# Input loaded and normalised in two token halves on two engines, and half of a lookup table made later, in a three-layer fused kernel on one Trainium2 core

## The reference

```
xn = _layernorm(x)                      # per token, over the 128 channels
x + attn_block(xn) + two_layers(xn)
# attn_block: group norm over all tokens, q k v, decayed retention in 16 heads of 8, output
#             projection, then group norm, 128 -> 256 -> 128 with silu
# each of two_layers (8 heads of 64):
h = shift_token(x); q, k, v = split(h @ wqkv)
q = l2norm(q) * q_scale; k = l2norm(k) * k_scale
q, k = rotary_xpos(q, k)                # cos, sin and a position scale
o = local_attention(q, k, v)            # window of 64 and the one before
x = x + o @ wo
h = layernorm(shift_token(x)); a, g = split(h @ w1 + b1); x = x + (a * gelu(g)) @ w2 + b2
```

## Time and profile before

| what | us |
|---|---|
| median of 3 runs | 972.21 |
| lowest and highest run | 970.54, 973.97 |
| span of the profiled execution, first to last instruction | 969.5 |
| TensorE busy | 862.3 (89%) |
| ScalarE busy | 701.7 (72%) |
| VectorE busy | 634.5 (65%) |
| GpSimd busy | 631.0 (65%) |

### The profile page before, as it was taken

One profiled execution on the slowest core, in us unless ns is written; L12 is line 12 of the kernel. 1 busy time (PEld: TensorE's weight loads), 2 busy tenths in 40 slices (PEclk: granted clock), 3 DMA queues, 4 the chain that ended last, 5 costly groups with the idle time before them and its releaser, 6 DMA issues.

```text
span 969.5 us, 26414 instructions
## 1 busy us (share of the span) xinstructions
PE 862.3 (89%) x10836; PEld 580.5 (60%) x10836; DVE 634.5 (65%) x1082; ACT 701.7 (72%) x1449; POOL 631.0 (65%) x500
## 2 busy tenths in 40 slices
PE   0678889989899898998999989999999999999876
PEld 0345666666667666666566656565656565656552
DVE  5874666666667567576575776757575758575632
ACT  0446786977868779677797778787878787878651
POOL 4588677675876758667586665757575758585700
PEclk9979999999999999999999999999999999999997
DMA  9100000000000000000000000000000000000000
GB/s 295 30 1 3 1 2 2 3 3 2 2 3 1 3 1 1 3 2 3 1 2 3 1 2 2 1 21 4 17 7 23 2 23 2 21 3 24 1 23 11
DMA packets 20482, 13.47 MB, mean 14 GB/s; under 512 B 4579, under 2 KB 19597, under 8 KB 20237
## 3 DMA queue, kind: packets, MB, share of 16 engines
q1 hardware_dynamic: 15108, 10.49, 3.6%
q10 hardware_dynamic: 5256, 1.31, 0.7%
HBM read 9.70 MB, written 2.10 MB: 12 GB/s over the span
## 4 chain that ended last, share of the span: by engine, by line
PE 63%; ACT 15%; DVE 10%; issue 7%; POOL 3%; DMA 1%; DVEq 0%; POOLq 0%; SPq 0%; ACTq 0%
PE pQK L1181 8%; PE pS L1108 6%; PE pT L1093 5%; PE pT L1050 5%; PE pM L1125 5%; PE pV L1146 4%; PE pS L1082 4%; PE pM L1254 4%; DVE m L734 4%; PE pT L1237 3%; PE pQK L1345 3%; PE pM L1119 2%; PE pS L1069 2%; ACT prT L545 2%; ACT pr L598 1%
## 5 line engine op out<-in xcount | busy, mean ns | idle before, releaser
L366 POOL TENSOR_TENSOR rn<-rn,half_neg 128x16 f32<-128x16 f32 x64 | 187.5, 2929 | 5.3
L379 POOL TENSOR_TENSOR m<-m 128x1024 f32<-128x1024 f32 x64 | 150.9, 2358 | 0.0
L364 POOL TENSOR_SCALAR rn<-ss 128x16 f32<-128x16 f32 x64 | 16.3, 254 | 193.3 <-DVE ss L747 192.1
L386 POOL TENSOR_TENSOR qkn<-m,rn 128x1024 f32<-128x1024 f32 x64 | 121.7, 1902 | 5.0
L1181 PE MATMUL pQK<-wqkv,hT 128*128 128x512 f32 x256 | 123.6, 606 | 0.9 <-DVE m L734 0.9
L780 DVE TENSOR_REDUCE mx<-pS 128x8 f32<-128x1024 f32 x64 | 78.1, 1220 | 63.8 <-PE pS L1082 63.8
L561 ACT ACTIVATE sq<-pQK 128x1024 f32<-128x1024 f32 x64 | 65.4, 1022 | 25.5 <-PE pQK L1181 25.4
L747 DVE TENSOR_REDUCE ss<-sq 128x16 f32<-128x1024 f32 x64 | 77.6, 1213 | 6.7 <-ACT sq L561 6.4
L782 DVE TENSOR_TENSOR pr<-pS,mx 128x1024 f32<-128x1024 f32 x64 | 78.4, 1225 | 2.2
L521 ACT ACTIVATE kT<-pT 128x512 f32<-128x512 f32 x64 | 38.0, 595 | 57.3 <-PE pT L1050 56.8
L545 ACT ACTIVATE prT<-pT 128x1024 f32<-128x1024 f32 x64 | 65.0, 1016 | 15.6 <-PE pT L1093 14.8
(11 more groups left out here) (169 smaller groups left out, 2015.9 us busy)
## 6 DMA issues: line engine op xcount, KB each, us to landing
x<-in_L_attn_x SPq DMA_DIRECT2D x4, 512.0 KB, 9.4
xs<-in_L_attn_x SPq DMA_DIRECT2D x8, 256.0 KB, 2.8
out<-aqkT SPq DMA_DIRECT2D x8, 256.0 KB, 2.2
wqkv<-in_L_ffn_wqkv SPq DMA_DIRECT2D x2, 768.0 KB, 9.8
tab<-in_k_tab SPq DMA_DIRECT2D x1, 1024.0 KB, 10.4
w<-in_L_ffn_w SPq DMA_DIRECT2D x2, 341.0 KB, 10.5
wo<-in_L_ffn_wo SPq DMA_DIRECT2D x2, 256.0 KB
cst<-in_k_cst ACTq DMA_DIRECT2D x1, 404.5 KB, 4.3
```

The lines of the kernel that those rows point to most:

```text
L366: eng.tensor_tensor(rn[:, k % 2, :], rn[:, k % 2, :], half_neg[:, 0:2 * H], ALU.pow).then_inc(S["rn_done"], 1)
L379: eng.tensor_tensor(m1[:, k % 2, :], m1[:, k % 2, :], m2[:, :], ALU.add).then_inc(S["add_done"], 1)
L386: eng.tensor_tensor(qkn[:, k % 2, :].rearrange("p (h d) -> p h d", d=DH), m1[:, k % 2, :].rearrange("p (h d) -> p h d", d=DH), rn[:, k % 2 ...
```

## The change

x is loaded in eight transfers instead of four: the first four steps of each batch, then the last four. VectorE takes the statistics of the first half, joins them, then those of the second half. GpSimd's two halves of 1/sqrt stay. VectorE also makes `shift` = -mean/std (L1002 in the changed kernel), so that ScalarE can normalise as Identity(x * rstd + shift): of each step ScalarE now normalises batches 0 and 1, VectorE batches 2 and 3. ScalarE's copy of step t-1 out of PSUM follows its normalisation of step t. Layer 1's rotary table is no longer made in the opening: its q part is made on GpSimd before slot 2 of body (0,1), its k part before slot 2 of body (0,2); its gains have a tile of their own, and VectorE waits for all twelve instructions only in body (1,0). The statistics of xnT move on VectorE from before slot 0 to before slot 1 of body (0,0). The opening's loops are written out.

The core of the diff:

```diff
-        gain = hidden[:, MASK_END:MASK_END + DEPTH * 2 * DH].rearrange("p (l g d) -> p l g d", l=DEPTH, g=2)
+        gain = [hidden[:, MASK_END:MASK_END + 2 * DH].rearrange("p (g d) -> p g d", g=2), sb("gain1", [P, 2, DH])]
...
         @block.sync
         def _(sp):
-            for b in range(NB):
-                sp.dma_start(x[:, b, :, :], a["L0_attn_x"][b].rearrange("(t p) d -> p t d", p=P)).then_inc(x_ld[b], 16)
+            for h in range(2):
+                for b in range(NB):
+                    steps = slice(h * NT // 2, (h + 1) * NT // 2)
+                    sp.dma_start(x[:, b, steps, :],
+                                 a["L0_attn_x"][b].rearrange("(t p) d -> p t d", p=P)[:, steps, :]).then_inc(x_ld[h][b], 16)
...
-            for l in range(DEPTH):
-                for g in range(2):
-                    eng.tensor_tensor(rope[l][:, :, g, :], tab[:, :, g, :],
-                                      gain[:, l, g, :].unsqueeze(1).broadcast_to([P, NT, DH]),
+
+            def rotary_table(l, g):
+
+                eng.tensor_tensor(rope[l][:, :, g, :], tab[:, :, g, :],
+                                  gain[l][:, g, :].unsqueeze(1).broadcast_to([P, NT, DH]),
+                                  ALU.mult).then_inc(rope_done, 1)
+                for s in range(2):
+                    eng.tensor_tensor(rope[l][:, :, 2 + g, 32 * s:32 * s + 32], tab[:, :, 2 + g, 32 * s:32 * s + 32],
+                                      gain[l][:, g, 32 - 32 * s:64 - 32 * s].unsqueeze(1).broadcast_to([P, NT, 32]),
                                       ALU.mult).then_inc(rope_done, 1)
-                    for s in range(2):
-                        eng.tensor_tensor(rope[l][:, :, 2 + g, 32 * s:32 * s + 32], tab[:, :, 2 + g, 32 * s:32 * s + 32],
-                                          gain[:, l, g, 32 - 32 * s:64 - 32 * s].unsqueeze(1).broadcast_to([P, NT, 32]),
-                                          ALU.mult).then_inc(rope_done, 1)
+            rotary_table(0, 0)
+            rotary_table(0, 1)
 
             def body(new, old, ff):
                 for k in range(NB):
                     if k == 1 and new and is_start(new):
                         pool_group_norm(eng, 0)
+                    if new in ((0, 1), (0, 2)) and k == 2:
+                        rotary_table(1, new[1] - 1)
                     if new == (1, 0) and k == NB - 1:
                         pool_group_norm(eng, 1)
                     pool_slot(eng, new, old, ff, k)
...
-            with eng.Fori(0, NT // 2) as half:
-                for u in range(2):
-                    t = 2 * half + u
-                    eng.wait_ge(xnt_mm, t + 1)
-                    eng.activation(xnT[:, :, bass.ds(t * P + 1, P)], xn_banks[u][:, :].rearrange("p (b n) -> p b n", b=NB),
-                                   ACT.Copy).then_inc(xnt_ev, 1)
+
+            def keep_transposed(t):
+                eng.wait_ge(xnt_mm, t + 1)
+                eng.activation(xnT[:, :, t * P + 1:t * P + 1 + P], xn_banks[t % 2][:, :].rearrange("p (b n) -> p b n", b=NB),
+                               ACT.Copy).then_inc(xnt_ev, 1)
+            for t in range(NT):
+                eng.wait_ge(rstd_done, t // (NT // 2) + 1)
+                eng.wait_ge(shift_done, t // (NT // 2) + 1)
+                need(eng, xnt_mm, t - 1)
+                for b in range(NB // 2):
+                    eng.activation(xn[:, t % 2, b, :], x[:, b, t, :], ACT.Identity, bias=shift[:, t, b:b + 1],
+                                   scale=rstd[:, t, b:b + 1]).then_inc(xn_act, 1)
+                if t > 0:
+                    keep_transposed(t - 1)
+            keep_transposed(NT - 1)
             eng.wait_ge(memset_done, 7 + 4 * NB)
...
-            for b in range(NB):
-                eng.wait_ge(x_ld[b], 16)
-                with eng.Fori(0, NT // 4) as quad:
-                    for u in range(4):
-                        t = 4 * quad + u
+            def row_stats(h):
+                for b in range(NB):
+                    eng.wait_ge(x_ld[h][b], 16)
+                    for u in range(NT // 2):
+                        t = h * (NT // 2) + u
                         eng.bn_stats(xst[:, b, t, :], x[:, b, t, :]).then_inc(xst_done, 1)
-            eng.wait_ge(xst_done, NB * NT)
-            for t in range(NT):
-                for b in range(NB):
-                    eng.bn_aggr(mv[:, t, b, :], xst[:, b, t, :]).then_inc(st_done, 1)
+
+            def join_stats(h):
+                eng.wait_ge(xst_done, NB * NT // 2 * (h + 1))
+                for u in range(NT // 2):
+                    t = h * (NT // 2) + u
+                    for b in range(NB):
+                        eng.bn_aggr(mv[:, t, b, :], xst[:, b, t, :]).then_inc(st_done, 1)
+
+            def row_shift(h):
+                steps = slice(h * NT // 2, (h + 1) * NT // 2)
+                eng.wait_ge(rstd_done, h + 1)
+                eng.scalar_tensor_tensor(out=shift[:, steps, :], in0=mv[:, steps, :, 0], scalar=-1.0, in1=rstd[:, steps, :],
+                                         op0=ALU.mult, op1=ALU.mult).then_inc(shift_done, 1)
+
+            def normalize(t):
+                need(eng, xnt_mm, t - 1)
+                for b in range(NB // 2, NB):
+                    eng.tensor_scalar(xn[:, t % 2, b, :], x[:, b, t, :], mv[:, t, b, 0:1], rstd[:, t, b:b + 1],
+                                      ALU.subtract, ALU.mult).then_inc(xn_done, 1)
+            row_stats(0)
+            join_stats(0)
+            row_stats(1)
+            row_shift(0)
+            join_stats(1)
             eng.wait_ge(cst_ld, 32)
             eng.tensor_copy(mask16[:, :], mask32).then_inc(mask_done, 1)
-            eng.wait_ge(rstd_done, 1)
-
-            def normalize(half):
-                for u in range(2):
-                    t = 2 * half + u
-                    need(eng, xnt_mm, t - 1)
-                    for b in range(NB):
-                        eng.tensor_scalar(xn[:, u, b, :], x[:, b, t, :], mv[:, t, b, 0:1], rstd[:, t, b:b + 1],
-                                          ALU.subtract, ALU.mult).then_inc(xn_done, 1)
-            for half in range(NT // 4):
-                normalize(half)
-            eng.wait_ge(rstd_done, 2)
-            with eng.Fori(NT // 4, NT // 2) as half:
-                normalize(half)
-            eng.wait_ge(rope_done, 6 * DEPTH)
+            for t in range(NT // 2):
+                normalize(t)
+            row_shift(1)
+            for t in range(NT // 2, NT):
+                normalize(t)
+            eng.wait_ge(rope_done, 6)
 
             def input_stats():
 
@@ -1018,11 +1048,12 @@
             def body(new, old, ff):
                 for k in range(NB):
                     if new and is_start(new):
-                        if k == 0:
+                        if k == 1:
                             input_stats()
-                        if k == 1:
                             bias_into_ffn()
                             dve_group_norm(eng, 0, c("ng"), c("nb"))
+                    if new == (1, 0) and k == 0:
+                        eng.wait_ge(rope_done, 6 * DEPTH)
                     if new == (1, 0) and k == 1:
                         eng.wait_ge(A["cs"], NB * NT)
                         dve_group_stats(eng, 1)
@@ -1363,17 +1394,13 @@
                     mm = eng.transpose(pT[:, g * 512 + j * P:g * 512 + (j + 1) * P], araw[:, 4 * g + j, :], ident)
                 mm.then_inc(awt_mm, 1)
 
-            def transpose_normalized(half):
-                for u in range(2):
-                    t = 2 * half + u
-                    eng.wait_ge(xn_done, 4 * t + 4)
-                    need(eng, xnt_ev, t - 1)
-                    for b in range(NB):
-                        mm = eng.transpose(xn_banks[u][:, b * P:(b + 1) * P], xn[:, u, b, :], ident)
-                    mm.then_inc(xnt_mm, 1)
-            transpose_normalized(0)
-            with eng.Fori(1, NT // 2) as half:
-                transpose_normalized(half)
+            for t in range(NT):
+                eng.wait_ge(xn_done, 2 * t + 2)
+                eng.wait_ge(xn_act, 2 * t + 2)
+                need(eng, xnt_ev, t - 1)
+                for b in range(NB):
+                    mm = eng.transpose(xn_banks[t % 2][:, b * P:(b + 1) * P], xn[:, t % 2, b, :], ident)
+                mm.then_inc(xnt_mm, 1)
 
```

More of the change, by code:

```diff
@@ L146, in program @@
         rstd = sb("rstd", [P, NT, NB])
+        shift = sb("shift", [P, NT, NB])
         cbst = [sb("cbst0", [P, NB, 2, 6]), sb("cbst1", [P, NB, NT, 6])]
@@ L226, in score_bank @@
             return pQK[:, 512 * (b % 2):512 * (b % 2) + 512]
-        x_ld = [sem(f"x_ld{b}") for b in range(NB)]
+        x_ld = [[sem(f"x_ld{h}_{b}") for b in range(NB)] for h in range(2)]
         cst_ld, tab_ld, aw_ld, wqkv_ld, w1_ld, w_ld, gain_ld, col_ld = (
@@ L232, in program @@
         memset_done, mask_done = sem("memset_done"), sem("mask_done")
+        xn_act, shift_done = sem("xn_act"), sem("shift_done")
```

(2 more changed lines are left out.)

## The result

The changed kernel took 975.53 us (median of 20 runs, 971.84 to 978.22) against 971.88 for the kernel before (20 runs beside it): ratio 1.0038, 95% interval 1.0028 to 1.0047. The forecast was 975.9. The profiled execution has a span of 972.5 (before 969.5) at a mean granted clock of 0.981 (0.983). It is slower, by little over what can be told from no change.

The account below looks back on a forecast made before the run. TensorE, busy 89% of the span, bounds the bodies; VectorE, slowed beside GpSimd, paces the opening. Span 969.5 - 2.6 + 2.6 + 3.7 = 973.2, plus 2.7 to the median: 975.9 us, range 970.6 to 978.3.

Parts of the forecast that it names:

- The opening, -2.6: Normalising on ScalarE and VectorE at 1.35 us a step starts hT at 38.4 instead of 40.97: -2.6 us.
- The halves, 0: Loads and statistics of x in halves gain 0 +-0.5 us, since ScalarE cannot normalise before about 26.45 anyway.
- The statistics, +2.6: Group norm statistics behind slot 0 of body (0,0) make TensorE wait, giving back the opening's 2.6 us; second ss at 58.7.
- rival C: Denser transposes raise TensorE's clock in the opening, 1.9 us sooner to second ss, table paid: 974.0 us; chance 0.15.
- The table, +3.7: Layer 1's table ahead of slot 2 delays ars by 1.90 us, costing 1.8 to 1.9 per body, 3.7 for both.
- Rival B: Table hidden, as VectorE and TensorE catch up inside the retention; opening and statistics cancel: 972.2 us; chance 0.20.
- Rival D: Statistics stay covered, opening's gain carried through, second ss before 57: 968.7 us with table hidden, 970.6 half paid; chance 0.13.
- E: Rival: the eight x transfers delay ScalarE's queue by 1 to 2 us: 977.5 us; chance 0.07.
- 2.7 between span and median: Whole run: the median run lies 2.7 us above the profiled span, added to 973.2 to give 975.9.
- A: The forecast itself: opening -2.6, statistics +2.6, table +3.7: 975.9 us, own range 974.3 to 977.8; chance 0.45.

Follow-up runs that it names:

- kernel 5: Changed kernel with the statistics of xnT back ahead of slot 0 and layer 1's table ahead of slot 1: 969.31 us, ratio 0.9956.
- Kernel 8: Changed kernel with x loaded by four transfers instead of eight halves, statistics still in eight steps: 976.70 us, ratio 1.0046.
- 11: kernel 9 with x loaded by four transfers instead of eight: 964.47 us, ratio 0.9913.
- kernel 9: kernel 5 with the eight bias column loads issued by SyncE, behind its weight loads, instead of by ScalarE: 959.13 us, ratio 0.9871.
- kernel 1: Changed kernel with the statistics of xnT put back ahead of slot 0 of body (0,0): 973.48 us, ratio 1.0017.
- kernel 3: Kernel before with only layer 1's table moved, to ahead of slot 2 of bodies (0,1) and (0,2): 972.58 us, ratio 1.0015.
- kernel 4: Kernel before with only layer 1's table moved, to ahead of slot 1 of bodies (0,1) and (0,2): 967.99 us, ratio 0.9953.
- 12: kernel 9 with VectorE's wait for layer 0's rotary table moved behind the eight statistics rows: 960.20 us, ratio 0.9871.
- kernel 2: Changed kernel with layer 1's table made ahead of slot 1, not slot 2, of bodies (0,1) and (0,2): 971.83 us, ratio 1.0000.

## Why the prediction was right

- **The opening, -2.6: right.** It won 2.53. The step of ScalarE was 1.29 (1.35 forecast), the queue ended 0.40 later than I took it, and the two errors nearly cancel. In the runs kernel 5, which has this opening without the two late costs, is 3.9 us below the kernel before of its group (2.6 to 5.9 by its interval).
- **The halves, 0: right, and shown.** Kernel 8, and 11 against 9, show the cover and what lies under it: the eight loads bring nothing while ScalarE's queue runs to 24.5, and 4 to 5 us when it ends at 12.6.
- **The statistics, +2.6: right in kind, small by 0.5.** The second `ss` came at 59.24, not 58.7, so all of the opening and 0.5 more was lost up to there, 3.0; undoing the move gave 2.33 in the trace of kernel 1 and 2.05 in the runs. I had `gst` at 56.1, and it was at 56.62. The 0.5 is TensorE's, not the move's: q and k of slot 0 took 3.62 us, 0.75 more than the 2.87 of the earlier trace rows, and some 0.2 of it came back behind. The changed kernel's timeline:

```profile
39.21 2.04 PE L1177 MATMUL pV<-wqkv,hT 128*128 128x512 f32 x2 [1.30 <-ACT hT L510]
41.05 3.62 PE L1212 MATMUL pQK<-wqkv,hT 128*128 128x512 f32 x4
44.46 2.57 PE L1413 MATMUL pM<-col,w 128*128 128x1 f32 x24
```

  They began 2.5 us earlier and took 0.9 each to their end, against 1.88 for four at 2.4 GHz, so they ran at the lower level (1.2 GHz), although the profile lists a granted clock of 1.00 for 41 to 44.7 us: the clock rose no sooner, which is rival C the other way round. But one trace can't lay this to the denser transposes. Kernels 3 and 4 are the same code up to body (0,1), and differ as much (first 3, then 4):

```profile
40.17 2.99 PE L1187 MATMUL pQK<-wqkv,hT 128*128 128x512 f32 x4
```

```profile
39.99 3.62 PE L1187 MATMUL pQK<-wqkv,hT 128*128 128x512 f32 x4
```

  With the two-engine opening it was 3.10 and 2.99 in kernels 9 and 12, and 3.56 to 3.62 in the other seven profiles. The Trainium skill (TensorE: Matmul & The Clock Gate, "What's actually happening") has the clock rise after sustained activity; in none of these nine profiles did the denser transposes ahead bring it for v and all of q, k. The row that GpSimd's `qkn` had held for 1.03 took 0.16, as forecast, but another one, ahead of it, took 0.62 instead of 0.15 (54.11), as I had allowed.
- **The table, +3.7: right.** GpSimd's 1.90 is in the changed kernel and in 3, `aqk` waits 1.92 longer, and moving the table off that slot gave 3.7 (2) and 4.6 (3 to 4). But I had each body 1.8 longer, and in the profile body (0,1) is 1.37 longer and body (0,2) 1.41 (62.72 against 61.31): of the 1.9 at slot 2, 0.5 is given back to waits further on. Against kernel 2, which has the table at slot 1, they are 2.01 and 1.25 longer. So the traces have 2.8 to 3.3 for both bodies, and the runs 3.7 and more; no run settles the difference, which is no larger than what executions differ by. Rival B, a table that costs nothing, is out.
- **Rival D is out** (second `ss` at 59.24, not before 57), and so is E (the queue 0.4 later, 0.27 by kernel 8, and kernel 8 no faster).
- **That the total hit to 0.4 us** is partly luck. The change itself was forecast as +3.7 on 972.21 and measured as +3.65 on 971.88. But the forecast's 2.7 between span and median is no fixed cost of a run, as I took it: in every execution listed with its span the time is 1.7 to 1.9 above it, so 0.9 of the 2.7 was that profile's being faster than its median. (And the upper end of the range, 978.3, is 0.5 above the 977.8 of A that it was to be taken from.) Executions of the changed kernel lie up to 3.7 us from their median, and the trace shows one reason. Windows of the changed kernel, 109 to 113 and 113 to 124 us (columns: span of the window, busy time of PE, PEld, DVE, ACT and POOL, granted clock, DMA share, GB/s):

```profile
109.00:113.00 4.00, 4.00 (x46) 3.36 (x45) 1.56 (x2) 1.07 (x2) 3.35 (x2) 0.57 0.02 4
113.00:124.00 11.00, 11.00 (x118) 7.89 (x117) 7.72 (x9) 9.09 (x15) 6.08 (x4) 1.00 0.00 1
```

  TensorE is busy throughout the first window, yet its granted clock is 0.57, so most of it lies at the lower level (1.2 GHz). Just ahead of it TensorE had stood still for 2.13 us:

```profile
108.21 1.10 PE L1177 MATMUL pV<-wqkv,hT 128*128 128x512 f32 x2 [2.13 <-DVE xr L821]
```

  The kernel before and kernel 2 stand still for the same 2.13 us there and keep 1.00. From `rn` of slot 0 to `rn` of slot 1 of body (0,1), the changed kernel fell 1.6 us further behind the kernel before. The window from 68 to 72, which follows an idle of 3.41 (3.15 before), has 0.57 after and 1.00 before; kernel 3 has 1.00 and kernel 4 falls to 0.50 behind the same idle of 3.40, and from slot 2 to slot 3 of body (0,0) kernel 4, the same code so far, loses 1.6 us on kernel 3. So whether the clock falls behind such an idle differs by execution, and a single trace is no measure of 1 or 2 us between kernels.
- **The point I passed by.** I read ScalarE's queue as the cover of the halves and costed it at nothing, but did not ask what the cover itself was worth: 10 us, the largest number in this study. The change shortened the work behind ScalarE's queue and left the queue, for whose end at 24.51 all of that work waited.

## What to carry to other kernels

When an edit is worth nothing because something hides it, price the cover: here eight loads of a kilobyte or less kept a compute engine's queue for 12 us, and moving them to an idle queue was worth nearly three times what the whole change moved. Work moved off a waiting engine's slack (the statistics before TensorE's 3 us wait) or onto a full one (the table at slot 2) must be placed by where the idle time stands at that instant: one slot earlier the same table left GpSimd 1.10 us to spare. What an edit is worth depends on the others: the eight loads were worth nothing behind a full queue and 4 to 5 us behind an empty one, and the empty queue was worth nothing on kernel 4 and 10 us on kernel 5. So undo edits one by one and in pairs.

## What the runs showed of the hardware

- Eight transfers of 1 KB or less took ScalarE's queue from 12.45 to 24.51 in the changed kernel, up to 3.44 us for one issue, with the DMA engines 96% busy over the first 30 us. Issued by SyncE from 22.79 in kernel 9, they took 4.6. The Trainium skill (DMA: Bandwidth & Descriptors, "Issuing engines are not separate DMA queues") says that spreading issues over engines saves only the sequencer's time, "usually small relative to the DMA itself". Issuing time is what was saved here, but it was not small: 12 us of an engine that had to compute.
- VectorE's rows beside GpSimd: a 128x4 product with two SBUF inputs took 1.02 to 1.03 us beside a running `qkn`, and 0.16 without; in the kernel before it ended with `qkn` (56.49 and 56.48). The Trainium skill (SBUF — State Buffer, "SBUF: two separate sides") describes an exclusive lock that VectorE and GpSimd share and that is held for a whole instruction, and this agrees. But the statistics rows ran at the same pace beside GpSimd and without it (4.84 for eight in both), so what moves beside GpSimd should be chosen by its kind.
